# Expert stages of a vision tower on one core: chunks taken two at a time on TensorE, gates of several chunks standing in projection banks, one VectorE multiply for each chunk

## The reference, cut to what matters

```python
# layer 0: one expert a token, hidden width 256, relu, with a capacity for each expert
hmid = relu(x @ w1[e] + b1[e]);  y_tok = (hmid @ w2[e] + b2[e]) * (prb * kept)
# layer 1: two experts a token, hidden width 64, gelu
out = tokens + sum_e combine[:, e] * (gelu(tokens @ w1[e] + b1[e]) @ w2[e] + b2[e])
# layer 2: two experts a token on a normalised input, hidden width 128, gelu
y = sum_e w_full[..., e] * (gelu(xn @ W1[e] + b1[e]) @ W2[e] + b2[e])
```

## Time and profile before

| | us |
|---|---|
| median of 3 runs | 192.59 |
| lowest and highest of them | 191.43, 195.23 |
| the profiled execution's own time | 191.28 |
| its span | 189.5 |
| PE busy | 161.5 (85%) |
| DVE busy | 106.3 (56%) |
| ACT busy | 69.2 (37%) |
| POOL busy | 28.6 (15%) |

### The profile page before, as it was taken

One profiled execution on the slowest core, in us unless ns is written; L12 is line 12 of the kernel. 1 busy time (PEld: TensorE's weight loads), 2 busy tenths in 40 slices (PEclk: granted clock), 3 DMA queues, 4 the chain that ended last, 5 costly groups with the idle time before them and its releaser, 6 DMA issues.

```text
span 189.5 us, 2926 instructions
## 1 busy us (share of the span) xinstructions
PE 161.5 (85%) x1134; PEld 73.7 (39%) x1134; DVE 106.3 (56%) x324; ACT 69.2 (37%) x117; POOL 28.6 (15%) x79
## 2 busy tenths in 40 slices
PE   1999949998999899788996969769889998999950
PEld 1244516443433344433452313236433344556410
DVE  6103993455555747576474899771764724103884
ACT  4604690473446110373420000333556046473121
POOL 6303200007776000001000000000029100000000
PEclk9999999999999999999999996999999999999995
DMA  6999900000000000000031000000000000000001
GB/s 192 360 424 282 324 1 0 0 3 2 2 0 5 0 0 0 0 3 0 0 48 51 0 0 0 0 0 3 0 3 0 0 2 3 0 0 3 0 0 31
DMA packets 4916, 8.26 MB, mean 44 GB/s; under 512 B 2747, under 2 KB 2875, under 8 KB 4774
## 3 DMA queue, kind: packets, MB, share of 16 engines
q1 hardware_dynamic: 4902, 8.07, 13.0%
HBM read 7.70 MB, written 0.37 MB: 43 GB/s over the span
## 4 chain that ended last, share of the span: by engine, by line
PE 54%; DVE 32%; DMA 5%; ACT 4%; issue 3%; POOL 0%; DVEq 0%; ACTq 0%; POOLq 0%
PE ps L427 8%; PE ps L369 7%; PE ps L414 7%; DVE scores L1173 5%; PE ps L421 3%; PE ps L487 3%; PE ps L383 3%; PE ps L376 3%; PE ps L751 2%; PE ps L478 2%; DVE hidden_gated L998 2%; DVE scores_rest L1184 2%; DMA k_scratch<-k_parts_tok 2%; DMA weights_sb<-weights 2%; DMA k_parts_img<-k_scratch 2%
## 5 line engine op out<-in xcount | busy, mean ns | idle before, releaser
L369 PE MATMUL ps<-idle_operand 128*128 128x512 bf16 x169 | 46.5, 395 | 5.8 <-DVE scores L1173 1.7
L998 DVE TENSOR_TENSOR hidden_gated<-hidden,ps 128x288 f32<-128x288 f32 x56 | 22.2, 450 | 14.5 <-PE ps L421 14.4
L787 ACT ACTIVATE hidden<-ps,weights_sb 128x576 f32<-128x576 f32 x28 | 20.2, 737 | 17.8 <-PE ps L414 15.3
L369 PEld LDWEIGHTS ps<-idle_operand 128*128 128x128 bf16 x169 | 14.6, 104 | 27.0 <-issue 8.3
L779 ACT ACT_TABLE_LOAD x16 | 20.5, 1283 | 0.3
L427 PE MATMUL ps<-hidden_gated,weights_sb 128*64 128x288 f32 x112 | 19.8, 432 | 0.8 <-DVE hidden_gated L998 0.8
L767 ACT ACTIVATE squares<-ps 128x288 f32<-128x288 f32 x8 | 3.3, 410 | 40.5 <-PE ps L427 10.2
L936 DVE COPY centred<-ps 128x288 f32<-128x288 f32 x8 | 3.7, 458 | 25.2 <-ACT squares L767 25.2
L297 POOL CAST combine_parts_T<-combine_parts_T 48x288 f32<-48x288 bf16 x3 | 1.3, 418 | 102.7 <-DVE combine_parts_T L970 102.7
L414 PE MATMUL ps<-h,weights_sb 64*128 64x288 f32 x80 | 14.4, 449 | 1.1 <-ACT hidden L787 0.8
L1173 DVE TENSOR_REDUCE scores<-ps 128x32 f32<-128x512 f32 (+1 forms) x15 | 8.8, 666 | 3.6 <-PE ps L621 3.6
(11 more groups left out here) (268 smaller groups left out, 230.8 us busy)
## 6 DMA issues: line engine op xcount, KB each, us to landing
patch_sb<-patches SPq DMA_DIRECT2D x6, 288.0 KB, 5.3
weights_sb<-weights SPq DMA_DIRECT2D x1, 1108.0 KB, 9.7
weights_sb<-weights SPq DMA_DIRECT2D x1, 717.0 KB, 14.3
weights_sb<-weights SPq DMA_DIRECT2D x1, 689.0 KB, 13.0
weights_sb<-weights SPq DMA_DIRECT2D x1, 640.0 KB, 7.4
weights_sb<-weights SPq DMA_DIRECT2D x1, 512.0 KB, 12.1
weights_sb<-weights SPq DMA_DIRECT2D x1, 394.0 KB, 13.0
weights_sb<-weights SPq DMA_DIRECT2D x1, 375.5 KB, 6.5
```

The lines of the kernel that those rows point to most:

```text
L369: mm(PS[:, bank, :], idle_in[:, 0:P], idle_in[:, :], start=True, stop=True)
L787: act.activation(HR[:, at % RING, :, :], two(ZA if ch % 2 == 0 else ZB), func, bias=w(f"b1_{n}")[:, ch:ch + 1]).then_inc(S["act_out"], 1)
L998: dve.tensor_tensor(HG[:, at % GRING, h, :], HR[:, at % RING, h, :], PS[:, G + h, 0:HALF], ALU.mult)\
```

## The change

- PE's order in the stages is written out. For n = 0, each pair of chunks of an expert is one block: its gate, the two `down`s of the pair before, and two `up`s. `early` is (2, 6), so six chunks are projected before the loop and not five.
- For n = 1 and n = 2 gates go not only to G, G+1 but also to the projection banks ZA, ZA+1 and ZB, ZB+1, once ACT has read what stood there. So up to three gates stand at once, and their matmuls don't wait for the chunk just before.
- A gate is signalled once for both halves, and it waits for a whole chunk. DVE multiplies a chunk of 128 x 576 in one instruction, and `gated` counts chunks.
- The two matmuls on a zero operand ahead of the transposes stay for n = 1 alone. For n = 2 `up(6)` stands between the transposes and the first gate.
- For n = 2 the broadcast from which DVE makes `HP` (L944, the helper `normalise`) goes to bank YB and not to G+1; DVE makes `HP` after it has copied the turned gates; the bias matmul is the first of the sum and waits for `HP`.

```diff
+        GATE_AT = {0: [G] * 2 * E, 1: [G, ZA, ZB, G], 2: [G, G, ZA, ZB, G, ZA, ZB, G]}
...
-                def gate(g, before):
+                def gate(g, bank, after=None):
+                    if after is not None:
+                        pe.wait_ge(S["gated"], BASE[n] + after + 1)
                     for h in range(2):
-                        if before > 0:
-                            pe.wait_ge(S["gated"], 2 * (BASE[n] + before - 1) + h + 1)
-                        mm(PS[:, G + h, 0:HALF], sel[:, g, h, :], CT3[:, :], start=True, stop=True)\
-                            .then_inc(S["gates"], 1)
+                        last = mm(PS[:, bank + h, 0:HALF], sel[:, g, h, :], CT3[:, :], start=True, stop=True)
+                    last.then_inc(S["gates"], 1)
...
-                    pe.wait_ge(S["gated"], 2 * (BASE[n] + ch) + 2)
+                    pe.wait_ge(S["gated"], BASE[n] + ch + 1)
...
+                def bias2(start):
+                    pe.wait_ge(S["ctf_ready"], n + 1)
+                    if n == 2:
+                        pe.wait_ge(S["hp"], 6)
+                    mm(psY, w(f"b2_{n}"), CTF[:, :], start=start, stop=False, skip_group_check=True)
+
+                early = {0: (2, 6), 1: (4, 4), 2: (6, 6)}[n]
...
-                idle(2, G)
+                if n == 1:
+                    idle(2, G)
...
+                if n == 2:
+                    up(6)
...
+                if n == 0:
+                    for pair in range(E):
+                        gate(pair, G, 2 * pair - 1 if pair > 0 else None)
+                        if pair == 0:
+                            bias2(True)
+                        else:
+                            down(2 * pair - 2)
+                            down(2 * pair - 1)
+                        for ch in (2 * pair + 6, 2 * pair + 7):
+                            if ch < chunks:
+                                up(ch)
+                    down(chunks - 2)
+                    down(chunks - 1)
+                elif n == 1:
+                    gate(0, G)
+                    pe.wait_ge(S["act_out"], BASE[1] + 3)
+                    gate(1, ZA)
+                    bias2(False)
+                    pe.wait_ge(S["act_out"], BASE[1] + 4)
+                    gate(2, ZB)
+                    gate(3, G, 0)
+                    for ch in range(chunks):
+                        down(ch)
+                else:
+                    gate(0, G)
+                    up(7)
+                    gate(1, G, 0)
+                    pe.wait_ge(S["act_out"], BASE[2] + 7)
+                    gate(2, ZA)
+                    bias2(True)
+                    pe.wait_ge(S["act_out"], BASE[2] + 8)
+                    gate(3, ZB)
+                    gate(4, G, 1)
+                    down(0)
+                    down(1)
+                    gate(5, ZA, 2)
+                    gate(6, ZB, 3)
+                    mm(psY, c("ident"), HP[:, :], start=False, stop=False, skip_group_check=True)
+                    down(2)
+                    down(3)
+                    gate(7, G, 4)
+                    for ch in range(4, chunks):
+                        down(ch)
...
-            broadcast(psBC, 0)
+            broadcast(psY, 0)
...
-                if n == 2:
-                    normalise(5, HP[:, :], "hp")
                 dve.wait_ge(S["comb_turned"], n + 1)
                 dve.tensor_copy(CT3[0:6 * E, :], psCT).then_inc(S["comb_t"], 1)
+                if n == 2:
+                    normalise(5, HP[:, :], "hp", psY)
...
-                    for h in range(2):
-                        dve.wait_ge(S["gates"], 2 * (GBASE[n] + gate_of(ch)) + h + 1)
-                        dve.tensor_tensor(HG[:, at % GRING, h, :], HR[:, at % RING, h, :], PS[:, G + h, 0:HALF], ALU.mult)\
-                           .then_inc(S["gated"], 1)
+                    dve.wait_ge(S["gates"], GBASE[n] + gate_of(ch) + 1)
+                    dve.tensor_tensor(HG[:, at % GRING, :, :], HR[:, at % RING, :, :], two(GATE_AT[n][ch]), ALU.mult)\
+                       .then_inc(S["gated"], 1)
```

More of the change, by code:

```diff
@@ L429, in down @@
                     last.then_inc(S["y_done"], 1)
-                early = {0: (2, 5), 1: (4, 4), 2: (6, 6)}[n]
+                def bias2(start):
[4 more added lines that the diff above has]
+                early = {0: (2, 6), 1: (4, 4), 2: (6, 6)}[n]
                 for ch in range(early[0]):
@@ L471, in ffn @@
-                down(chunks - 1)
+                if n == 0:
[41 more added lines that the diff above has]
+                        down(ch)
@@ L785, in hidden @@
                     if at >= RING:
-                        act.wait_ge(S["gated"], 2 * (at - RING) + 2)
+                        act.wait_ge(S["gated"], at - RING + 1)
                     act.activation(HR[:, at % RING, :, :], two(ZA if ch % 2 == 0 else ZB), func,
@@ L939, in variance, with normalise @@
                 dve.reciprocal(RS[:, 0:n], SD[0:TT, 0:n]).then_inc(S["rs"], 1)
-            def normalise(k, dst, sem):
+            def normalise(k, dst, sem, spread=psBC):
                 dve.wait_ge(S["bc"], k + 1 if k < 5 else k + 2)
-                dve.tensor_tensor(dst, XC[:, :], psBC, ALU.mult).then_inc(S[sem], 1)
+                dve.tensor_tensor(dst, XC[:, :], spread, ALU.mult).then_inc(S[sem], 1)
             def col(x, p, n):
```

## The result

The changed kernel takes 186.59 us in the median of 5 runs (185.17 to 186.71), the kernel before 192.59 in the median of 5 (191.43 to 195.23; two runs came to the three shown ahead). The ratio is 0.972, with a 95% interval of 0.968 to 0.976: faster by 2.8%. It leaves out executions in a slower state, and so it is not the quotient of the two medians, 0.969. The profiled execution of the changed kernel took 185.17 us with a span of 183.4, for 191.28 and 189.5 before.

What follows compares the result with a forecast made beforehand. PE was taken to bound stage 0, and the loop gate, multiply, next gate the stages' ends. Gains of 2.43 + 1.09 + 2.88 = 6.40 us made 191.28 into 184.9; 185.5 was forecast, allowing for the median's spread, range 183.6 to 188.6.

Steps and rivals of the forecast that it cites:

- The sum: Gains of 2.43, 1.09 and 2.88 us in stages 0, 1 and 2, in all 6.40 us; forecast's chance 0.60.
- The price of a `down` behind a `down`: On PE, a second `down` in a row adds 0.48 us, between bounds of 0.46 and 0.64.
- The first rival: `down` behind `down` gains nothing (0.64 us); total gain 4.73 us, 186.6 us, up to 187.9; chance 0.15.
- The second: Rival: PE's order gains nothing, a stage 0 block stays 3.01 us; total gain 3.70 us, 187.6 us; chance 0.12.
- The block of 2.64: Each full block of stage 0 on PE: gate 0.35, two `down`s 1.12, two `up`s 1.17 us.
- DVE's loop: Stage 0's end, gate to gate with whole-chunk multiplies: 0.53 + 1.44 + 0.04 = 2.01 us.
- today's 1.95: The loop gate to gate by halves in the kernel before, taken as 0.40 + 1.55 us.
- Stage 1: DVE's four multiplies take 2.80 us with no gate late; the square comes at 90.77 for 91.86, gain 1.09 us.
- Stage 2: With the zero matmuls gone and gates in free banks, the last `down` starts at 148.80 for 151.68, gain 2.88 us.
- the new wait of chunk 6 for `down(2)`: Stage 2: DVE's chunk 6 waits for a ring place until 146.65; over some 0.5 us would show the forecast wrong.
- DVE waiting for gates in the middle of stage 0: Sign that the forecast is wrong: DVE's L998 waits for gates there; no size given.
- The third rival: PE's clock falls at stage 0's start without zero matmuls, blocks take 5.28 us, total 195.5 us; chance 0.04.

Runs made afterwards that it cites:

- experiment 1: Changed kernel with stage 0's order alone undone (gate, down, up, down, up): stage 0 26.48 us, median 186.58 us.
- Experiment 2: Changed kernel with multiplies and signals by halves again, PE's order and banks kept: median 184.42 us, ratio to the kernel before 0.959.
- experiment 3: Changed kernel with the gates of stages 1 and 2 in bank G alone, each after the previous chunk's multiply: median 191.23 us, ratio 0.992.
- Experiment 7: No zero matmuls from the end of stage 0 on: 200.40 us for the changed kernel, 209.02 us for the kernel before, one execution each.

## Why the prediction was right

**The sum.** 6.40 us was forecast on the profiled execution's 191.28, that is 184.9; the profiled execution took 185.17. By stage: 2.43 forecast and 2.35 measured, 1.09 and 1.12, 2.88 and 2.75. The time on record was 185.5, the median 186.59, inside the range of 183.6 to 188.6. The miss is in the step from one execution to the median: the profiled execution was again the lowest of its runs, 0.8% under the median, and the forecast had gone only half that way.

**The price of a `down` behind a `down`.** Taken as 0.48 by likeness with `up`, between bounds of 0.46 (from rows at half speed) and 0.64; measured 1.12 - 0.64 = 0.48. The first rival falls with it. The second falls with the two `up`s at 1.17 in the middle of the stage, and experiment 1 shows that the order makes the difference. The block of 2.64 came out to the hundredth. The rule on changing modes that the text weighed (the Trainium skill, "TensorEngine Tiling (Array Packing)", "Key Properties") agrees with experiment 1's 3.00 against 2.64 for the same instructions. No run changes the mode alone, so what is shown is the price of alternating these two kinds of matmul, and not its cause inside the engine.

**DVE's loop.** 2.01 was forecast, 2.04 measured. But the comparison with today's 1.95 was wrong. It counted the loop by halves as all four multiplies, while the next gate's first half waits only for the third. The kernel before did have 1.94 between its last two gates, but for another reason:

```profile
60.67 0.42 PE L421 MATMUL ps<-combine_parts_T,selectors 128*128 128x288 bf16 x2
...
61.97 0.71 PE L427 MATMUL ps<-hidden_gated,weights_sb 128*64 128x288 f32 x4 [0.25 <-DVE hidden_gated L998]
```

A `down` waited for the second multiply, and the gate stood behind it on PE until 62.61. That the two figures agree is luck. Experiment 2 shows the halves' loop as 1.70 once PE's order lets it. So the whole-chunk multiply was booked as a gain in DVE's work and a loss of 0.06 in the loop; in stage 0 it costs 0.67. The sum was untouched, since it was made from the changed kernel's own times.

**Stage 1.** DVE's chain was named as what is late next, 2.80 forecast, 2.75 measured. The gates were never late.

**Stage 2.** The first gate behind `up(6)`, `HP` under cover, the new wait of chunk 6 for `down(2)` are all in the timeline. That wait took 0.58 us. The text named one of over some 0.5 as a sign of being wrong, though its own times give 0.62: chunk 5 is done at 142.02 + 0.53 + 0.76 + 4 x 0.68 = 146.03, `down(2)` at 146.65. So this sign could not tell. Nor could DVE waiting for gates in the middle of stage 0: it waits 1.22 us for each there, as it waited 1.45 before, since PE is the bound. From the transposes to the second gate it took 2.29 us for 2.23 forecast, to the last `down` 9.1 for 9.0.

**The clock.** The third rival did not come: in the profiled execution of the changed kernel the clock is 1.00 in all three stages, without the zero matmuls that the change takes out of stages 0 and 2. That a half clock would eat up the gain is borne out by the 27.58 us of stage 0 in experiment 3, but there the fall lies ahead of the changed code. Experiment 7 took out other zero matmuls, those between the stages above all, and lost 14 to 16 us. The warning of the Trainium skill ("TensorE: Matmul & The Clock Gate", "Why this matters for your kernels") agrees in kind with experiment 7 and doesn't touch this change.

## What to carry to other kernels

Where TensorE is the bound and its matmuls alternate between shapes, put those of one shape behind each other: here it took the same instructions from 3.00 to 2.64 us a block. Where two engines take turns, break the loop with another buffer first; a coarser instruction saves work (a pair of chunks 1.42 us for 1.55) but makes the loop longer (2.04 for 1.70), and here it was free in stage 0 only when the loop was gone. Compare by the length of stages when the median varies by as much as the effect.

## What the hardware showed that was not expected

- The second of two like matmul pairs (four records of 288 columns, fp32) costs 0.48 us, for 64*128 and for 128*64 alike; one between others costs 0.64 to 0.69.
- Runs of one kernel spread over up to 5.9 us (189.67 to 195.61 in experiment 3, mean granted clock 0.993 and 0.958). In the profiles with the lowest mean clock that keep their zero matmuls (0.952 to 0.960), PE's granted clock falls to 0.50 at about 34 us, ahead of the changed code. It is open what starts this fall.
- Zero matmuls that stand in nobody's way are worth 13.8 and 16.4 us here (one execution of each kernel against the medians); the two pairs that stood ahead of the transposes cost 0.54 us each.
